# Self-attention with the exponentials divided by their sums ahead of transposition

## The reference

```
xn     = layernorm(x; g1, b1);  q, k, v = split(xn @ sa_wqkv)
wei    = softmax(where(causal, q k^T * C**-0.5, -inf) + padding, axis=-1)
result = x + (wei v) @ sa_wproj + sa_bproj
q2     = layernorm(result; g2, b2) @ ed_wq;  k2, v2 = split(layernorm(ctx; g2, b2) @ ed_wkv)
result = result + softmax(q2 k2^T * C**-0.5) v2 @ ed_wproj + ed_bproj
result = result + relu(layernorm(x; g3, b3) @ ff_w1 + ff_b1) @ ff_w2 + ff_b2
```

## Time and profile before

| | |
|---|---|
| time, median of 3 runs | 1353.91 us (1353.34 to 1354.88) |
| the profiled execution's own time | 1354.59 us |
| its span | 1351.6 us |
| TensorE busy | 1298.9 us, 96% |
| VectorE, ScalarE, GpSimd busy | 58%, 49%, 52% |
| self-attention | from 339.8 us to 683 us of the span |

### The profile page before, as it was taken

The page is one execution under the profiler, slowest core; times in us unless marked ns, Lnnn a source line. Parts: engine busy times, 40 slices in busy tenths (PEclk is TensorE's granted clock), DMA queues, the critical chain, the costliest instruction groups (busy, mean ns, idle before and its releaser), DMA issues.

```text
span 1351.6 us, 24602 instructions
## 1 busy us (share of the span) xinstructions
PE 1298.9 (96%) x9193; PEld 1073.3 (79%) x9193; DVE 787.7 (58%) x2003; ACT 663.1 (49%) x1611; POOL 701.2 (52%) x582
## 2 busy tenths in 40 slices
PE   6999999999999999999898999999999999999997
PEld 6888888888878888888686787878878787787874
DVE  6612222223677787777645565756657575675565
ACT  5411111222666766566625465574645647465444
POOL 3233131323434564458653767585666757666661
PEclk9999999999899999999998999999999999999999
DMA  7400102113657575697576667768677578766641
GB/s 238 141 28 16 63 32 71 42 60 112 128 155 207 146 178 143 171 225 202 159 138 124 116 91 119 132 119 140 89 137 118 101 130 131 120 99 111 91 72 42
DMA packets 102128, 160.06 MB, mean 118 GB/s; under 512 B 10389, under 2 KB 63421, under 8 KB 100730
## 3 DMA queue, kind: packets, MB, share of 16 engines
q1 hardware_dynamic: 102010, 158.50, 55.8%
HBM read 70.93 MB, written 28.31 MB: 73 GB/s over the span
## 4 chain that ended last, share of the span: by engine, by line
PE 77%; POOL 9%; DVE 6%; issue 3%; ACT 3%; DMA 2%; SPq 0%; POOLq 0%; ACTq 0%; DVEq 0%
PE ps L1778 17%; PE ps L164 12%; PE ps L453 11%; PE ps L423 10%; PE ps_pair L1795 6%; PE ps L1810 5%; PE ps L1824 5%; POOL ca_partial L1640 4%; PE ps L1887 3%; POOL ca_xT L1519 2%; PE ps L1246 1%; PE ps L1266 1%; PE ps L1842 1%; PE ps_pair L1236 1%; DMA ca_k_stack<-ca_keys 1%
## 5 line engine op out<-in xcount | busy, mean ns | idle before, releaser
L1717 DVE TENSOR_REDUCE ca_maxes<-ps 112x1 f32<-112x375 f32 x512 | 255.8, 539 | 111.9 <-PE ps L1810 110.1
L1640 POOL TENSOR_TENSOR ca_partial<-ca_partial,ca_probT 125x896 f32<-125x896 f32 x118 | 249.5, 2114 | 93.3 <-ACT ca_probT L1661 88.7
L1661 ACT ACTIVATE ca_probT<-ps_pair 125x448 f32<-125x448 f32 x384 | 207.2, 553 | 178.6 <-PE ps_pair L1795 177.6
L312 POOL TENSOR_TENSOR ff_hT<-ff_hrelu,ff_hT 128x512 fp32r<-128x512 f32 (+1 forms) x64 | 78.7, 1232 | 203.5 <-DVE ff_hT L394 203.5
L1795 PEld LDWEIGHTS ps_pair<-ca_q_stack,ca_k_stack 98*125 98x125 f32 x768 | 129.2, 186 | 49.8 <-issue 29.4
L1810 PE MATMUL ps<-ca_k_stack,ca_q_stack 96*112 96x376 f32 x512 | 164.6, 350 | 4.0 <-DVE ca_mrow L1745 2.1
L1795 PE MATMUL ps_pair<-ca_q_stack,ca_k_stack 98*125 98x224 f32 x768 | 158.1, 288 | 3.9 <-ACT ca_probT L1661 3.8
L423 PE MATMUL ps<-ff_w,ff_hT 128*128 128x512 f32 x672 | 155.5, 390 | 0.0
L1778 PE MATMUL ps<-ca_xT,w_a 128*128 128x376 f32 x768 | 153.8, 336 | 0.2 <-issue 0.2
L1778 PE MATMUL ps<-w_b,ca_xT 128*125 128x512 f32 x576 | 151.0, 398 | 0.4 <-DVE ca_keys L1766 0.4
L423 PEld LDWEIGHTS ps<-ff_w,ff_hT 128*128 128x128 f32 x672 | 125.6, 188 | 25.8
(11 more groups left out here) (144 smaller groups left out, 2377.5 us busy)
## 6 DMA issues: line engine op xcount, KB each, us to landing
ca_k_stack<-ca_keys SPq DMA_DIRECT2D x96, 376.0 KB, 8.0
sa_Q_stack<-sa_rows SPq DMA_DIRECT2D x96, 112.0 KB, 3.6
sa_K_stack<-sa_rows SPq DMA_DIRECT2D x96, 112.0 KB, 3.7
ca_q_stack<-q_out SPq DMA_DIRECT2D x96, 112.0 KB, 9.5
ctx_tokens<-in_ctx_dram SPq DMA_DIRECT2D x14, 672.0 KB
ctx_tokens<-in_L_xattn_ff_w_dram SPq DMA_DIRECT2D x16, 512.0 KB, 4.3
q_out<-sa_yT SPq DMA_DIRECT2D x16, 448.0 KB, 4.1
wp_lo<-wp_out SPq DMA_DIRECT2D x6, 1024.0 KB, 4.9
```

What stands on the lines that cost most here:

```text
L1640: pool.tensor_tensor(total, total, half(a), ALU.add).then_inc(partial_done, 1)
L1661: act.activation(probT[u // GH][0:JT, u % GH].rearrange("p a t -> p (a t)"), ps_p[u % 2][0:JT, 0:2 * T], ACT.Exp).then_inc(exp_done, 1)
L1717: dve.tensor_reduce(maxes[:, q, j, a:a + 1], ps_s[n % 3][0:TQ, 0:JH], AX_X, ALU.max).then_inc(s_read, 1)
```

## The change

Each head's exponentials are divided by their sums in place, between `exp` and the transposition: for even heads VectorE multiplies by the reciprocal (two `tensor_tensor` with the reciprocal broadcast), for odd heads ScalarE does (two activations with the reciprocal as scale). The reciprocals are taken once per head on VectorE. The transpositions of the reciprocals, the copies around them and the multiplication of the product are gone; the value product is read from PSUM by ScalarE (high part) and VectorE (remainder), one slot after it. LAG goes from 2 to 3, and some fills change places.

```diff
-LAG = 2
+LAG = 3
-FILLS = {0: [("Y", -2, 1)], 1: [("Y", -2, 2)], 2: [("V", 0, 0)], 3: [("V", 0, 1)], 4: [("Y", -2, 3)], 5: [("P", -1, 0)],
-         6: [("Q", 1, 0)], 7: [("P", -1, 1)], 8: [("K", 1, 0)], 9: [("Q", 1, 1)], 10: [("K", 1, 1)], 11: [("Q", 1, 2)],
+FILLS = {0: [("Y", -2, 1)], 1: [("Y", -2, 2)], 2: [("Y", -2, 3)], 3: [("V", 0, 0)], 4: [("V", 0, 1)], 5: [("P", -1, 0)],
+         6: [("P", -1, 1)], 7: [("Q", 1, 0)], 8: [("K", 1, 0)], 9: [("Q", 1, 1)], 10: [("K", 1, 1)], 11: [("Q", 1, 2)],
          12: [("K", 1, 2), ("R", -1, 0)], 13: [("Q", 1, 3), ("R", -1, 1)], 14: [("K", 1, 3)], 15: [("Y", -1, 0)]}
...
+        if 0 <= n - 1 < 16 * B:
+            items.append(("recip", n - 1))
         items += reads[n]
         if b < B:
             items.append(("exp", n))
-        if (n - LAG) % 4 == 2 and 0 <= n - LAG < 16 * B:
-            items.append(("recip", (n - LAG) // 4))
+        if 0 <= n - 1 < 16 * B:
+            items.append(("divide", n - 1))
         items += rests[n]
...
             items.append(("value", G))
-            reads[n + 1].append(("sums_read", G))
-            rests[n + 1].append(("scale", G))
-            reads[n + 2].append(("scale_hi", G))
-            rests[n + 2].append(("scale_lo", G))
+            reads[n + 1].append(("output_hi", G))
+            rests[n + 1].append(("output_lo", G))
...
-            if i in (3, 4):
-                items.append(("T", b + 1, i - 3))
-                rests[n + 1].append(("T_split", b + 1, i - 3))
+            if i in (4, 5):
+                items.append(("T", b + 1, i - 4))
+                rests[n + 1].append(("T_split", b + 1, i - 4))
... ScalarE
+        if name == "divide" and item[1] % 2 == 1:
+            n = item[1]
+            act.wait_ge(inv_done, n + 1)
+            for q in range(2):
+                row = prob[:, n % 4, TQ * q:TQ + T * q]
+                ins = act.mul(row, row, inv[:, n % 4, q:q + 1])
+            ins.then_inc(odd_divided, 1)
-            act.copy(rinv_T[:, G % 2], ps_o[G % 2][:, T:2 * T]).then_inc(rinvT_done, 1)
...
-            act.copy(oT[:, HI, G % KT], of[:, G % 2]).then_inc(ohi_done, 1)
+            act.copy(oT[:, HI, G % KT], ps_o[G % 2][:, 0:T]).then_inc(ohi_done, 1)
... VectorE
-            dve.wait_ge(exp_done, GH * (G + 1))
-            dve.reciprocal(inv[:], sums[:, G % 2]).then_inc(inv_done, 1)
-            dve.wait_ge(inv_done, G + 1)
-            dve.tensor_copy(rinv[:, G % 2].rearrange("p q (j d) -> p q j d", d=HD),
-                            inv[:].unsqueeze(3).to_broadcast([TQ, 2, GH, HD])).then_inc(recip_done, 1)
-        if name == "scale":
...
+            dve.wait_ge(exp_done, n + 1)
+            dve.reciprocal(inv[:, n % 4], sums[:, n % 4]).then_inc(inv_done, 1)
+            if n % 2 == 0:
+                dve.wait_ge(inv_done, n + 1)
+                for q in range(2):
+                    row = prob[:, n % 4, TQ * q:TQ + T * q]
+                    ins = dve.tensor_tensor(row, row, inv[:, n % 4, q:q + 1].to_broadcast([TQ, TQ * (q + 1)]), ALU.mult)
+                ins.then_inc(even_divided, 1)
+        if name == "output_lo":
...
-            dve.tensor_tensor(oT[:, LO, G % KT], of[:, G % 2], oT[:, HI, G % KT].bitcast(F32),
+            dve.tensor_tensor(oT[:, LO, G % KT], ps_o[G % 2][:, 0:T], oT[:, HI, G % KT].bitcast(F32),
                               ALU.subtract).then_inc(olo_done, 1)
... TensorE
-            pe.wait_ge(exp_done, n + 1)
+            pe.wait_ge(odd_divided if n % 2 else even_divided, n // 2 + 1)
...
-                pe.wait_ge(of_done, G - 1)
+                pe.wait_ge(olo_done, G - 1)
...
-            pe.wait_ge(recip_done, G + 1)
-            for q in range(2):
-                pe.transpose(o[:, T + TQ * q:T + TQ * (q + 1)], rinv[:, G % 2, q, :], ident)
```

More of the change, by code:

```diff
@@ L840, in self_attention @@
     maxes = sb("maxes", [TQ, 4, 2], F32, 87296)
[L841 to L845, removed]
+    sums = sb("sums", [TQ, 4, 2], F32, 87328)
+    inv = sb("inv", [TQ, 4, 2], F32, 87392)
     oT = sb("oT", [P, 2, KT, T], F32R, 142336)
@@ L860, in self_attention @@
         sem(n) for n in ("causal_ready", "mask_ready", "mask_half", "masks_ready", "bias_added"))
[L861 to L864, removed]
+    s_psum, max_done, inv_done = (sem(n) for n in ("s_psum", "max_done", "inv_done"))
+    even_divided, odd_divided = sem("even_divided"), sem("odd_divided")
+    exp_done, t_psum, o_psum, probT_done = (
+        sem(n) for n in ("exp_done", "t_psum", "o_psum", "probT_done"))
+    ohi_done, olo_done = sem("ohi_done"), sem("olo_done")
     t_read, hi_done, thi_done = sem("t_read"), sem("hi_done"), sem("thi_done")
@@ L1068, in scalar @@
             n = item[1]
-            h = n % H
             act.wait_ge(max_done, n + 1)
@@ L1073, in scalar @@
                                      ACT.Exp, bias=maxes[:, n % 4, q:q + 1], scale=-1.0,
-                                     accum_out=sums[:, (n // GH) % 2, q, h % GH:h % GH + 1])
+                                     accum_out=sums[:, n % 4, q:q + 1])
             ins.then_inc(exp_done, 1)
-        if name == "sums_read":
+        if name == "divide" and item[1] % 2 == 1:
[5 more added lines that the diff above has]
+            ins.then_inc(odd_divided, 1)
+        if name == "output_hi":
             G = item[1]
             act.wait_ge(o_psum, G + 1)
-            act.copy(rinv_T[:, G % 2], ps_o[G % 2][:, T:2 * T]).then_inc(rinvT_done, 1)
-        if name == "scale_hi":
-            G = item[1]
-            act.wait_ge(of_done, G + 1)
             if G % KT == 0 and G > 0:
                 wait_psum(act, ("P", G // KT - 1, 1))
-            act.copy(oT[:, HI, G % KT], of[:, G % 2]).then_inc(ohi_done, 1)
+            act.copy(oT[:, HI, G % KT], ps_o[G % 2][:, 0:T]).then_inc(ohi_done, 1)
         if name == "round_y":
@@ L1299, in self_attention @@
                      "query_stacks": (stacked["Q"][KT - 1], STACKED * B), "key_stacks": (stacked["K"][KT - 1], STACKED * B), "maxima": (max_done, H * B), "probabilities": (probT_done, H * B),
-                     "scaled": (of_done, KT * B), "value_products": (o_psum, KT * B), "results": (fin_done, B),
+                     "scaled": (olo_done, KT * B), "value_products": (o_psum, KT * B), "results": (fin_done, B),
                      "results_stored": (res_stored, 16), "prepared_weights": (wo_stored, 32 * len(prepared)),
```

## The result

The changed kernel takes 1363.95 us (median of 4 runs, 1362.48 to 1367.63) against 1354.39 (4 runs): ratio 1.0076, 95% interval 1.006 to 1.0092. It is slower by 9.6 us where 1349 was forecast. Its profiled execution took 1367.63 (span 1365.8), 3.7 above its own median, at a mean granted clock of 0.988 where its other three runs had 0.990 and 0.991; that of the kernel before took 1354.59 (span 1351.6, 0.992).

The account below looks back on a forecast made before the run. TensorE, busy 96%, was taken as the bound, VectorE second at 75%. Six batch periods gain 7.8, later first P costs 0.6, clock 2.3: -4.9 on 1354.6 gives 1349.7, median 1349; range 1339 to 1364.

Parts of the forecast that it names:

- 1337 + 2.3 for the clock: Rival, VectorE keeps up: unstretched divisions, periods of 39.1, 1337 us without the clock's fall, charged 2.3; chance 0.17.
- 17.4 - 7.8: Gains over six batch periods: 17.4 us with VectorE's divisions unstretched, 7.8 us in the forecast.
- on the path: TensorE: the reciprocals' two transpositions go in 32 groups, 9.0 to 11.2 us, all counting unless another engine takes TensorE's place.
- hidden: ScalarE: odd heads' divisions add 4.3 us a batch to 25.8 to 28.6 of 41, costing no time.
- narrow stretch: Twelve slots in a row with 224-column fills, 7 to 2 of the next batch; TensorE predicted to wait 1.6 us a batch.
- c: Time by which GpSimd stretches an even head's pair of VectorE divisions beyond its 0.51 us; taken as 0.3 a pair.
- wide stretch: Slots 3 to 6, V, V, P, P together, 3.29 us of TensorE a slot; VectorE has time to spare and catches up.
- The walk: Slot-by-slot sum of VectorE's queue, score 7 to value product in slot 3: 27.0 us against TensorE's 25.4.
- the point of decision: Stretching of a VectorE division pair from which the slower rival decides: 0.3 + 4.9 / 36 = 0.44.
- VectorE becomes the bound: Slower rival: GpSimd stretches VectorE's division pairs by 0.7, not 0.3, adding 14.4 us, 1363; chance 0.27.
- Moved items: Fills Q 0, T and P 1 change slots, no DMA added: nothing beyond what the VectorE queue sum includes.
- the clock's fall at the first V of batch 1: Idle TensorE drops to its lower clock, 1.2 instead of 2.4 GHz, once more there: 2.3 us charged, at most 2.9.

Follow-up runs that it names:

- the other two pairs: ScalarE's divisions left out: of the changed kernel, 1363.95 to 1360.3; of the changed kernel with even heads' reciprocals in PSUM, 1354.61 to 1350.29.
- PSUM version: Changed kernel with the even heads' reciprocals written to PSUM instead of SBUF, so VectorE's divisions have one SBUF input: 1354.61 us, ratio 0.9993.

## Why the prediction was wrong, step by step

Subtracting the runs from one another gives each part a price, to set beside the prediction's (each includes what the clock did in it, and each can be off by a microsecond or two):

| part | predicted | measured | from |
|---|---|---|---|
| all but the divisions | 1339.3 | 1344.7 | 1337 + 2.3 for the clock; run without divisions |
| ScalarE's divisions | 0 | 3.1 | 1347.8 - 1344.7 (3.7 and 4.3 in the other two pairs) |
| VectorE's, unstretched | 0 | 6.8 | 1354.6 - 1347.8 |
| their stretching | 9.6 | 9.3 | 17.4 - 7.8; 1364.0 - 1354.6 |
| sum | 1349 | 1364 | |

**The transpositions: the first step that failed.** 9.0 to 11.2 us were said to be all "on the path". Before, a slot with a value product took 0.43 + 0.07 + 0.28 = 0.78 up to that product; without a wait it takes 0.59 now: 0.19 saved, in 32 groups 6.1. The row that misled is the earlier trace rows: 0.28 start to start is what the two transpositions occupy, but they also covered a gap of 0.16 between a slot's transpositions and its value product. This gap appears when they go; no releaser stands beside it, and its cause was not tried. And in the order before, nothing at all comes of it (1.0005): by the waits VectorE takes TensorE's place, the prediction's own condition, and the clock has its part.

**ScalarE "hidden": failed.** It costs 3.1 to 4.3. Its busy time, 25.8 to 28.6 of some 42 us and the 4.3 added, was read as room. In the changed kernel 3.3 us of it can be followed: an odd division stands in ScalarE's queue ahead of the reading L1132, and a slot with a 224-column fill takes TensorE only 1.85 us, so it is soon back for a free PSUM tile: 0.54 in either batch looked at, in the same slot, 3.8 in all, and nearly gone with the divisions. In the other two pairs this wait is missing or 0.9, and the profiled executions hardly differ (spans 1346.0 and 1346.1, 1349.6 and 1348.5, for medians 3.1 and 4.3 apart): where the price arises there stays open. LAG 3 protects the transposition, the only reader thought of, in the narrow stretch: one wait of 0.3 for L1078 from 380 to 655 us. Outside it doesn't: from 340 to 740 there are four waits, 4.1 us, one of 1.17 just ahead of the first V; before, that window had three waits for the exponentials, 2.7 us. The longer wait, 1.35 for L1130, is another matter: there it stands behind the 2.05 us of the prepared weights on ScalarE, it doesn't go with the divisions, and it counts in the first row of the table.

**VectorE's divisions in themselves: put at nothing, the largest price, and only in part located.** At c = 0 the prediction had VectorE in the narrow stretch at 25.2 against TensorE's 25.4, thus for nothing. With c = 0 in fact (reciprocals in PSUM), the divisions still cost 6.8. It is not the narrow stretch of an ordinary batch that pays. The window of the run without VectorE's divisions beside the PSUM version's 40.77:

```profile
508.50:549.03 40.53, 40.10 (x348) 35.17 (x346) 28.32 (x121) 29.78 (x108) 22.05 (x30) 1.00 0.66 189
```

VectorE has 4.2 us less to do, and the period is 0.24 shorter. Less the 13.4 of the wide stretch (38.8 - 25.4), the narrow one takes 27.1 to 28.5 in both, two to three more than TensorE's 25.4, with the divisions or without: that is in the first row of the table. The two profiled executions differ by 3.6 us of span: 1.9 ahead of the first P, where the PSUM version's first V ran at the lower clock (4.35 us in place of 3.02); 1.5 in batch 6, where VectorE has the context's statistics; 0.6 in the five other periods; 0.5 less behind. The rest of the 6.8 is in neither trace (the PSUM version's profiled execution, 1351.34, is the second shortest of twelve): it stays open.

**The walk,** score 7 to the value product in slot 3, predicted 27.0, is 481.91 to 511.85 = 29.9 in the batch shown. The six slots with pairs come to 1.3 more than predicted in sum, the two ends to 0.4; slot 14 took 5.9 instead of 4.55 (1.35 idle, not 0.5; the splitting 1.32, not 1.21; weights and mask 2.1, not 1.8). The rest of the period, 43.3 - 29.9 = 13.4, is as predicted. So the bound was placed right and its length wrong. The pairs there were 0.58, 1.66, 1.05, 0.58, 1.26 and 1.50 start to end, 6.2 in sum from start to next start: in this stretch c is 0.52.

**Stretching: mis-sized in c, right in time by two errors that cancel.** c was 0.43 and not 0.3, close to the 0.4 that was worked out by the page of the Trainium skill and to the 0.44 named as the point of decision; what it cost, 9.3, is what 0.3 had been charged with. Of the four periods in which both executions had the full clock three show it as well: 43.30, 43.34 and 42.35 against 41.74, 41.72 and 40.77, 1.6 each (batch 6: 44.01 against 43.37). So each microsecond of c cost less than the walk says; the waits that the walk lacked may hide part of it, which no run tried. The rule of the Trainium skill (SBUF — State Buffer, section Who interferes with whom) that a VectorE instruction with at most one SBUF input, outside the two-port modes, does not contend with GpSimd agrees with the longest division of 0.382 us instead of 2.203. The rival "VectorE becomes the bound" gave 1363 and 1364 came, with periods of 43.7. It got there with c = 0.7 at 36 us for each microsecond of c; measured, c = 0.43 cost 9.3, or 22 for each, and other terms made up the difference. That the number agrees does not make the mechanism whole.

**Moved items: "nothing" failed.** At LAG 2 the moves alone cost 8.7. At LAG 3 the same moves gain 10, so what they cost in the changed kernel can't be read off by subtraction. The error of 5.4 in the table's first row contains it, together with the gap above and the 3.4 us of added waits for L1130. Which of GpSimd's wait of 11.4 us and of the twelve narrow slots in a row does the harm at LAG 2 stays open.

**Right:** the clock's fall at the first V of batch 1 (V took 4.74 in place of 3.03, the value product ahead of it 1.35 in place of 0.78: 2.3, as charged), the LAG in the narrow stretch, the waits for the division and the copy, and the test "wrong if periods are 42 or more", which decided. The other two falls in the profiled execution were not foreseen; that execution is 3.7 above the median, and by their granted clock the other runs hold less of them.

## What to carry to other kernels

Before work is moved from a full engine to one that is busy 75%, walk the densest stretch only and charge every queue that the work joins, the third engine's too: each reader behind the new instruction can be the one that TensorE waits for. Leave out one part at a time, here each engine's divisions: that sized in one run each what the sum had at nothing. Compare the profiled executions as well as the medians before a price is given a place: here some prices of the medians were in neither trace. An instruction that goes from a queue saves only what its removal leaves uncovered; look for the latency that it was covering.

## What the runs showed of the hardware

A reciprocal in PSUM as the second input frees a VectorE multiplication of GpSimd's blocking at no cost in its floor (0.270 against 0.274 us); the form with one tensor input and a pointer, all in SBUF, is blocked as long as the other (2.175 us). For a copy whose only input moved to PSUM the floor did rise (0.423 against 0.293 us). How much the blocking costs depends on the place: 128 instructions lost 37.7 + 31.5 - 24.4 - 17.3 = 27.5 us of VectorE's time, of which 9.3 reached the end.
